# SiLU as one ACT function instead of tanh and products on DVE and POOL, in a fused decoder layer of 16 groups

## The reference

```python
# 1. attention layer: a gated state-space layer, 16 heads, then a small memory
proj = rmsnorm(x) @ w_in.T            # val (256), gate (256), B and C (16 heads x 128), dt (16)
val  = silu(depthwise_conv4(val))     # a causal convolution of four taps over tokens
ld   = softplus(dt) * -exp(A_log)     # cum = cumsum(ld)
M    = (C @ B.T) * exp(cum_l - cum_m) # per head, lower triangle
Y    = M @ val + D_skip * val
out  = Y * silu(gate) @ w_out.T       # then a decayed linear memory over out, layer norm
# 2. cross attention over ctx (softmax with a mask), two layer norms
# 3. feed-forward with quantised weights and activations
h = act_quant(x) @ ternary(w1).T      # 512 hidden channels
h = silu(depthwise_conv3(h))
y = act_quant(h) @ ternary(w2).T      # act_quant needs the largest |h| of each token
x = layernorm(x + y)
```

## Time and profile before

| | |
|---|---|
| median of 3 runs | 895.32 us (894.7 to 895.62) |
| profiled execution, own time | 894.32 us |
| its span on the core | 892.2 us |
| busy: PE, DVE, ACT, POOL | 803.7, 779.4, 695.7, 194.9 us |
| granted TensorE clock | 0.953 of full speed on average |

### The profile page before, as it was taken

One profiled execution on the slowest core, in us unless ns is written; L12 is line 12 of the kernel. 1 busy time (PEld: TensorE's weight loads), 2 busy tenths in 40 slices (PEclk: granted clock), 3 DMA queues, 4 the chain that ended last, 5 costly groups with the idle time before them and its releaser, 6 DMA issues.

```text
span 892.2 us, 21288 instructions
## 1 busy us (share of the span) xinstructions
PE 803.7 (90%) x7928; PEld 589.3 (66%) x7928; DVE 779.4 (87%) x2286; ACT 695.7 (78%) x1372; POOL 194.9 (22%) x237
## 2 busy tenths in 40 slices
PE   3899999999999999999999999999999999966431
PEld 3667677777777677777777776777777777634221
DVE  4565679999999999999999999999999999897755
ACT  2786788888889898898888898988888888754432
POOL 6300013121220313131212202131313121223121
PEclk9899999999999999999999999999999999998555
DMA  6311110211020211110210202011111101000000
GB/s 188 74 18 25 25 37 14 49 33 17 26 48 26 46 28 37 38 37 14 57 16 30 44 25 47 27 38 36 37 25 47 17 28 34 21 18 12 0 12 24
DMA packets 51586, 30.64 MB, mean 34 GB/s; under 512 B 40442, under 2 KB 42444, under 8 KB 51484
## 3 DMA queue, kind: packets, MB, share of 16 engines
q1 hardware_dynamic: 51052, 28.17, 13.8%
q10 hardware_dynamic: 432, 1.11, 0.4%
HBM read 16.68 MB, written 4.19 MB: 23 GB/s over the span
## 4 chain that ended last, share of the span: by engine, by line
PE 51%; DVE 26%; ACT 10%; issue 6%; SPq 2%; POOL 1%; DMA 1%; ACTq 0%; POOLq 0%; DVEq 0%
PE pM L2384 6%; PE pP L2334 5%; PE pP L2336 4%; PE pP L2335 4%; DVE fa L1778 3%; DVE hm L1795 3%; PE pDec L2371 3%; DVE fa L1780 2%; PE pDec L2368 2%; DVE u L1786 2%; ACT L771 2%; DVE ML L1658 2%; DVE conv L1604 2%; PE pC L2507 2%; PE pC L2478 2%
## 5 line engine op out<-in xcount | busy, mean ns | idle before, releaser
L2334 PE MATMUL pP<-xn_hi,G_hi 128*128 128x256 f32 x512 | 157.9, 308 | 1.0 <-ACT P L746 1.0
L746 ACT ACTIVATE P<-pP 128x512 f32<-128x512 f32 x256 | 148.1, 598 | 11.6 <-PE pP L2336 10.5
L2335 PE MATMUL pP<-xn_lo,G_hi 128*128 128x256 f32 x512 | 144.0, 281 | 0.0
L2336 PE MATMUL pP<-xn_hi,G_lo 128*128 128x256 f32 x512 | 143.8, 281 | 0.0
L2384 PE MATMUL pM<-P,xnT 128*64 128x512 f32 x512 | 133.7, 597 | 0.3
L2334 PEld LDWEIGHTS pP<-xn_hi,G_hi 128*128 128x128 f32 x512 | 97.3, 190 | 18.0 <-issue 10.3
L2335 PEld LDWEIGHTS pP<-xn_lo,G_hi 128*128 128x128 f32 x512 | 97.7, 191 | 3.2 <-issue 0.7
L1658 DVE TENSOR_TENSOR ML<-pM,Lm 128x512 f32<-128x512 f32 x128 | 87.6, 684 | 14.0 <-PE pM L2384 11.6
L2336 PEld LDWEIGHTS pP<-xn_hi,G_lo 128*128 128x128 f32 x512 | 97.2, 190 | 0.0
L604 POOL TENSOR_TENSOR rs_c<-ve_c,half_pow 128x4 f32<-128x4 f32 x48 | 48.5, 1011 | 197.8 <-DVE nm_c L1750 100.9
L595 POOL TENSOR_TENSOR u<-u,fa 128x512 f32<-128x512 f32 x32 | 40.8, 1276 | 226.3 <-ACT u L846 226.3
(11 more groups left out here) (240 smaller groups left out, 2055.2 us busy)
## 6 DMA issues: line engine op xcount, KB each, us to landing
v_nat<-vT SPq DMA_DIRECT2D x256, 32.0 KB, 2.1
x_in<-in_x SPq DMA_DIRECT2D x16, 256.0 KB, 2.8
x_res<-in_x SPq DMA_DIRECT2D x16, 256.0 KB, 2.6
ctxT<-in_ctx_t SPq DMA_DIRECT2D x16, 256.0 KB, 3.0
out_x<-x SPq DMA_DIRECT2D x16, 256.0 KB, 2.0
P<-in_wc ACTq DMA_DIRECT2D x2, 512.0 KB, 6.6
P<-in_wb SPq DMA_DIRECT2D x2, 512.0 KB, 9.0
fa<-in_w_t SPq DMA_DIRECT2D x1, 256.0 KB
```

The lines of the kernel that those rows point to most:

```text
L746: act.activation(P[:, half, 2 * pair:2 * pair + 2, 0:w], pP[k % 2][:, 0:2 * w].rearrange("p (h l) -> p h l", h=2), ACT.Copy).then_inc(p_co ...
L2334: pe.matmul(dst, w_hi, x_hi, start=True, stop=False)
L2335: pe.matmul(dst, w_hi, x_lo, start=False, stop=False)
L2336: return pe.matmul(dst, w_lo, x_hi, start=False, stop=True)
```

## The change

- The three tanh steps on ACT become SiLU steps in the same places and of the same shapes: `value_silu` and `gate_silu` and `ffn_silu` are now ACT functions that call `ACT.Silu`.
- `value_silu` and `gate_silu` on DVE, and `ffn_silu` on POOL and on DVE, are gone, with the semaphores between.
- `conv` has two buffers, one for each jj; `fa` has four, one for each c. The waits of `conv_bias` and `ffn_bias` for a free buffer are gone. `ha` is gone: `hidden_abs` writes into `fa`, which is then free.
- The constants 0.25 and 0.5 are gone (two small steps of the setup on DVE), and 2e-5 becomes 1e-5.
- `decay_exp`, the softmax and the softplus keep their functions.
- The call lists of all engines are written anew: `fill()`, `body(g)` and `drain()` hold the remaining calls in another order.

```diff
-        conv = sb("conv", [128, GS, L])
+        conv = sb("conv", [128, JJ, GS, L])
-        fa = sb("fa", [128, 2, GS, L])
+        fa = sb("fa", [128, FB, GS, L])
...
-            def ffn_silu(d, c):
-                pool.wait_ge(f_tanh.sem, f_tanh.at(d, c + 1))
-                silu(ch_u, d, u[:, c, 0:late_width(d)], flat(fa[:, c % 2, 0:late_seqs(d), :])).then_inc(u_most_ready.sem, 1)
...
-            def value_tanh(n, jj):
+            def value_silu(n, jj):
                 act.wait_ge(a_read.sem, a_read.at(n, A_VAL[jj]))
...
-                act.activation(vT[n % 2][:, jj, 0:width(n)], flat(conv[:, 0:seqs_in(n), :]), ACT.Tanh, scale=0.5)\
-                   .then_inc(val_tanh.sem, 1)
+                act.activation(vT[n % 2][:, jj, 0:width(n)], flat(conv[:, jj, 0:seqs_in(n), :]), ACT.Silu)\
+                   .then_inc(vT_ready.sem, 1)
...
-                act.activation(gT[n % 2][:, jj, 0:width(n)], pA[:, 0:width(n)], ACT.Tanh, scale=0.5).then_inc(gate_tanh.sem, 1)
+                act.activation(gT[n % 2][:, jj, 0:width(n)], pA[:, 0:width(n)], ACT.Silu).then_inc(a_read.sem, 1)
...
             def ffn_bias(d, c):
                 act.wait_ge(d_mm.sem, d_mm.at(d, D_H + c))
-                if c >= 2:
-                    act.wait_ge(u_most_ready.sem, u_most_ready.at(d, c - 1))
...
-            def ffn_tanh(d, c):
+            def ffn_silu(d, c):
                 act.wait_ge(d_read.sem, d_read.at(d, D_H + c))
-                act.activation(u[:, c, 0:late_width(d)], flat(fa[:, c % 2, 0:late_seqs(d), :]), ACT.Tanh, scale=0.5)\
-                   .then_inc(f_tanh.sem, 1)
+                act.activation(u[:, c, 0:late_width(d)], flat(fa[:, c, 0:late_seqs(d), :]), ACT.Silu)\
+                   .then_inc(u_ready.sem, 1)
...
-            def ffn_silu(d, c):
-                dve.wait_ge(f_tanh.sem, f_tanh.at(d, c + 1))
-                hidden = u[:, c, 0:late_width(d)]
-                dve.scalar_tensor_tensor(hidden, hidden, 1.0, flat(fa[:, c % 2, 0:late_seqs(d), :]),
-                                         ALU.add, ALU.mult).then_inc(u_last_ready.sem, 1)
```

More of the change, by code:

```diff
@@ L1068, in fill @@
+                copy_p(2, 1, 3)
+                copy_p(2, 1, 4)
+                ffn_bias(0, 1)
+                decay_exp(2, 4)
+                ffn_silu(0, 0)
                 copy_p(2, 1, 5)
+                ffn_bias(0, 2)
+                copy_p(2, 1, 6)
                 conv_bias(3, 1)
-                copy_memory_values(1)
-                ffn_tanh(0, 0)
-                copy_p(2, 1, 6)
-                ffn_bias(0, 1)
+                hidden_abs(0, 0)
                 copy_p(2, 1, 7)
-                decay_exp(2, 4)
@@ L1090, in fill @@
                 hidden_abs(0, 2)
+                copy_p(3, 0, 1)
+                gate_silu(3, 0)
+                value_silu(3, 1)
+                ffn_silu(0, 3)
+                copy_queries(1)
+                copy_p(3, 0, 2)
+                gate_silu(3, 1)
+                hidden_abs(0, 3)
+                decay_exp(2, 5)
+                attention_exp(1)
                 copy_p(3, 0, 3)
-                ffn_tanh(0, 3)
-                copy_queries(1)
-                gate_tanh_step(3, 1)
@@ L1279, in drain @@
                 hidden_abs(10, 2)
+                gate_silu(13, 0)
+                copy_p(13, 0, 2)
+                ffn_silu(10, 3)
+                copy_queries(11)
+                value_silu(13, 0)
+                value_silu(13, 1)
+                hidden_abs(10, 3)
+                gate_silu(13, 1)
+                decay_exp(12, 5)
+                attention_exp(11)
                 copy_p(13, 0, 3)
-                ffn_tanh(10, 3)
-                copy_queries(11)
-                gate_tanh_step(13, 1)
@@ L1322, in drain @@
-                ffn_bias(11, 1)
-                decay_exp(13, 3)
-                ffn_tanh(11, 1)
-                copy_p(13, 1, 6)
-                copy_p(13, 1, 7)
-                decay_exp(13, 4)
-                ffn_bias(11, 2)
+                ffn_silu(11, 1)
+                copy_p(13, 1, 6)
+                ffn_bias(11, 2)
+                copy_p(13, 1, 7)
+                hidden_abs(11, 0)
+                conv_bias(14, 1)
+                hidden_abs(11, 1)
+                first_apply(12)
@@ L1404, in drain @@
+                ffn_silu(12, 3)
+                gate_silu(15, 0)
+                hidden_abs(12, 3)
+                copy_queries(13)
+                gate_silu(15, 1)
+                decay_exp(14, 5)
+                attention_exp(13)
+                copy_p(15, 0, 2)
+                copy_weights(13)
                 copy_p(15, 0, 3)
-                ffn_tanh(12, 3)
-                copy_queries(13)
-                gate_tanh_step(15, 1)
-                hidden_abs(12, 3)
+                place_cum(15)
@@ L1447, in drain @@
[L1447 to L1449 removed]
                 ffn_bias(13, 3)
+                ffn_silu(13, 2)
                 copy_x1T(14)
@@ L1997, in body @@
-                softmax_sum(g - 2)
-                hidden_scale(g - 3)
-                last_norm(g - 4)
-                second_norm(g - 2)
-                decayed(g - 1, 7)
-                hidden_int(g - 3, 0)
+                decayed(g - 1, 4)
+                add_skip(g - 1, 0)
+                hidden_max(g - 3, 2)
+                gate_y(g - 1, 0)
+                hidden_max(g - 3, 3)
+                below_maximum(g - 2)
+                decayed(g - 1, 5)
+                hidden_scale(g - 3)
@@ L2150, in drain @@
-                hidden_scale(11)
-                last_norm(10)
-                second_norm(12)
-                decayed(13, 7)
-                hidden_int(11, 0)
+                x1_shifted(12)
+                cum_low(14)
+                decayed(13, 4)
+                hidden_max(11, 1)
+                add_skip(13, 0)
+                hidden_max(11, 2)
+                rms_stats(15)
+                hidden_max(11, 3)
+                below_maximum(12)
+                decayed(13, 5)
+                hidden_scale(11)
@@ L2708, in fill @@
-                scores(1, 6)
-                attend(0)
-                v_transposed(2, 0)
-                decay(1, 7)
+                cum_transposed(2)
+                head_values(1, 2)
+                head_values(1, 3)
+                head_pair(2, 0, 4)
+                decay(1, 6)
+                head_pair(2, 0, 5)
+                weights_transposed(0)
+                v_transposed(2, 0)
+                head_pair(2, 0, 6)
+                attend(0)
+                decay(1, 7)
+                scores(1, 6)
```

1932 lines of the change are left out of this document (898 added, 1034 removed).

## The result

The changed kernel takes 916.21 us, median of 4 runs (914.83 to 917.62); the kernel before, on the same chip, 895.07 us (894.7 to 895.62). The ratio is 1.0236, 95% interval 1.0216 to 1.0255: 21 us slower, where 26 us faster had been forecast. The profiled execution took 917.13 us, its span 915.3.

What follows compares the result with a forecast made beforehand. The prediction took DVE to bound the steady part at 48.8 us a group, PE close behind. Gains of 16.3 (steady periods), 0.6 (first groups) and 9.0 (end) made 25.9 us: span 866.3, time 869 us, range 857 to 887.

Steps and rivals of the forecast that it cites:

- What bounds the kernel before: Steady part: DVE is the bound, its list takes 48.8 us a group with 0.2 us of waits; the change frees 3.6.
- I cost it at nothing in the period beyond the loads: ACT's new order: about 16.5 us without decay factors, taken as covered by other work of PE and DVE.
- Cost of the function: ACT: a SiLU takes the tanh's time, 634 ns; ACT's need goes from 42.9 to 45.7 us with the loads.
- Cost of a load: ACT: two more table loads a group, 1.28 us each, 1.4 with lost overlap, 2.8 us together.
- The period, 47.6 forecast: Steady groups: period falls from 48.96 to 47.6 us, 1.36 in each of 12 periods, 16.3 us.
- 0.9 us of waits: PE, steady period: the part of its 2.3 us of waits let stay, a choice between bounds 0 and 2.3.
- the 46.7 that the prediction gave PE: PE's need per steady period, read by starts: 44.8 us of spacings plus 1.9 for changes of kind.
- The end: Last groups' open feed-forwards: 9.0 us gained, of which group 15 gives 4.2 by its last maximum coming earlier.
- the 4.8 us for groups 14 and 13: The end: 2.1 us from group 14's earlier root and norm, 2.7 from group 13's moved norm and dropped product.
- PE as the bound: Rival, steady part: PE needs near its busy 48.2, period 48.3 or more, about 880 us; chance 0.2.
- A switch of 2.6 us: Rival, ACT: a drain makes each table switch 2.6 us, period at least 49, time 892 us; chance 0.02.
- ACT as the bound (the slower one): Rival, steady part: ACT keeps its 6.1 us of waits, period 51.8, about 920 us, spread 897 to 920; chance 0.09.

Runs made afterwards that it cites:

- e3: Kernel before with its old call lists, products removed and buffers added, Tanh in place of SiLU (no SiLU computed): 878.74 us, ratio 0.983.
- e4: Changed kernel with half of the 16 transfers of v of a group issued by POOL instead of SP: 896.6 us, ratio 1.0031.
- e5: e4 with POOL issuing its half of the v moves ahead of its power for the next group's statistics: 887.53 us, ratio 0.9911.
- e7: Changed kernel with the first value SiLU of groups 13 and 14 moved sooner in ACT's drain list, no split of the moves: 903.27 us, ratio 1.0089.
- e9: Changed kernel with both repairs: POOL issues half the v moves ahead of its power, first value SiLU of groups 13 and 14 sooner: 878.39 us, ratio 0.9821.
- e6: e5 with Tanh in place of Silu (no SiLU computed), 36 fewer table loads: 884.95 us, ratio 0.9881.
- e2: Kernel before with its old call lists, products removed and buffers added, Silu on ACT, 150 table loads: 1017.38 us, ratio 1.1378.
- e8: e2 with three calls a step moved in ACT's list to group the SiLUs, for 5 loads a group: 963.33 us, ratio 1.076.
- e10: e9 with the third head product left out in the first half of each group, less PE work: 871.71 us, ratio 0.9744.
- e15: e9 with the third head product left out in both halves, and taps, biases and absolute values on half of the columns: 835.52 us, one run.
- e13: e9 with DVE's fourteen tap operations a group on half of the columns: 870.11 us, one run.
- e14: e9 with ACT's biases and absolute values on half of the columns: 872.27 us, one run.

## Why the prediction was wrong, point by point

- **What bounds the kernel before: half right.** DVE's 0.2 us of waits did mean that relief of DVE shortens the period: with the products and their buffer waits gone and no call moved (e3) it went from 48.95 to 47.93. But DVE's 3.6 us gave only 1.0.
- **"I cost it at nothing in the period beyond the loads": the step that failed.** I named the risk of the new order rightly as an order's, and looked for it in one place, the decay factors. I didn't follow what the moved SiLUs release: `value_silu` hands to SP 8 issues of 0.64 us a half, and the last lands 2.1 later. Where both halves come together these are 12.4 us between the second SiLU and `v_transposed`, where PE had left some 7. This is 33.0 us of waits in the trace, and repairing it alone (e4, e5, e7, e9: no work removed) took the ratio from 1.0236 to 0.9821, 37 us. The queue of SP was in no sentence of the prediction, nor in a rival. By section, gain forecast against gain measured: start 0.6 and -13.4, eight steady periods 10.9 and 1.7, groups 12 to 14 4.1 and -16.7, the rest 10.4 and 5.2. Of the 49 us between forecast and result 35 lie in the start and in groups 12 to 14, where the long waits for v are.
- **Cost of the function: right.** A SiLU is 600 to 631 ns where the tanh was 590 to 635, so this trace agrees with the Trainium skill's rule of one element a cycle whatever the function ("ScalarE: Activation LUTs", "What ACT_TABLE_LOAD costs"). ACT's need of 45.7 was 45.2.
- **Cost of a load: right as an engine's time, wrong as a cost.** The row is 1.28 us as before. What a load costs in time depended on its place: some 0.07 us each by the medians and 0.15 by the periods with the moves in time (e5 against e6), 1.2 to 1.3 each in the old order (e2 and e8 against e3), where PE then waited for ACT.
- **The period, 47.6 forecast: mis-sized.** 48.78 measured; with v in time 48.29, with tanh 47.98. The sum took the largest need of an engine and let 0.9 us of waits stay. e10 to e15 show that the period isn't the largest need plus a remainder: it was 1.6 us over the 46.7 that the prediction gave PE, with each engine idle a little. The 46.7 itself looks low: PE's busy time is 47.54 in a period of e6, of e13 and of e14, and e13's period of 47.53 has no gap on PE. Over the twelve periods e9's 48.29 for 47.6 is 8 of the 9 us by which even e9 is behind the forecast.
- **The end: group 15 right, the rest mis-sized.** From the first tap to the end of the last maximum it was 12.96 us before; it is 8.97 now (888.30 to 897.27), 4.0 less against 4.2 forecast, with the eight taps in a row as described. Of the 4.8 us for groups 14 and 13 little came: from the mark of group 15 to that first tap 1.1 us were gained, of which the period alone should have given 1.4.
- **The rivals.** PE as the bound gave a period of 48.3 and 880 us, near e9's numbers and not by its mechanism. A switch of 2.6 us is not it: in group 13 ACT ends an instruction at 663.10, loads, and starts the next at 664.41, 1.31 in all. ACT as the bound (the slower one) is not it: ACT had a wait of 7.1 us for PE in group 13. That 916 lies within that rival's 897 to 920 is luck: it had the right sign from the wrong queue. 0.10 for everything of that sign was too little where every list is written anew and only one hand-over of it had been followed.

## What to carry to other kernels

When work moves within a list, follow what its end releases, up to the consumer: the transfers behind it with their issue time each, and who else is in that queue. Issues of 0.6 us are nothing one by one and a critical path sixteen at a time; if producers come closer together, the issuing queue can become the bottleneck, although nothing was added to it. Where the queue is late, spread its issues over idle engines, and ahead of their own waits: e4 without that care gave 18 us, e5 with it 29. The Trainium skill ("Trainium Kernel Development and Optimization", "Key Constraints") says that issuing from several engines "only saves the sequencer's issue time"; the runs agree, and here that was 29 us, more than the whole loss of 21.

Second, three engines over 90% busy behaved here as one chain. Don't forecast a period as the largest need: a cut on one engine gave about a quarter of itself here, whichever engine it was.

## What the runs showed of the hardware

- A small transfer of `move_v` (32 KB) occupies SP's queue for 0.60 us and the next starts 0.64 after it; POOL issues the same in 0.53 us (8 in 4.2, e4). From issue to landing it is 2.1 us on SP (median, 2.0 to 3.5).
- A wait of 7.0 us on PE is followed by 4.6 us at a granted clock of 0.51, starts 0.21 apart in place of 0.12. So a late operand cost about 9 us for 7 (e7: with waits 6.0 and 4.2 us shorter in groups 13 and 14 their periods are 7.5 and 6.5 shorter).
- A Silu between Exps needs a load each way (71 loads where Tanh has 35), at 1.28 us and some hundredths around it (1.31 for the switch in group 13).
